# A hybrid convolution, attention and routed feed-forward block: the early plan over two slots, gelu's splits ahead of the weight splits, four batches of picks

## The reference

```python
x = x + _L0_conv_ref(_gn(x), t, weights1, ke_weights, ke_bias)   # group norm, 16 Fourier modes of the channels mixed
t = _to_tokens(x)                                                # 16 sequences of 256 tokens
t = t + _L1_attn_ref(_ln_t(t), W_q, W_k, W_v, W_o)               # causal attention, one head of 256
t = t + _L1_ffn_ref(_ln_t(t), router_w, w_fc, w_proj)

def _L1_ffn_ref(x, router_w, w_fc, w_proj):
    router_probs = jax.nn.softmax(flat_x @ router_w, axis=-1)    # 8 experts
    topk_w, topk_idx = jax.lax.top_k(router_probs, 2)
    topk_w = topk_w / jnp.sum(topk_w, axis=-1, keepdims=True)
    ...
    for e in range(E):
        h = jax.nn.gelu(flat_x @ w_fc[e], approximate=False)     # 256 -> 1024
        out = out + combine[:, e:e + 1] * (h @ w_proj[e])        # 1024 -> 256
```

## Time and profile before

| What | us or share |
|---|---|
| median of three runs | 695.71 |
| profiled execution, its own time | 695.76 |
| its span | 693.9 |
| TensorE (PE) busy | 618.7 (89%) |
| VectorE (DVE) busy | 491.0 (71%) |
| ScalarE (ACT) busy | 412.4 (59%) |
| GpSimd (POOL) busy | 399.6 (58%) |

### The profile page before, as it was taken

The page is one execution under the profiler, slowest core; times in us unless marked ns, Lnnn a source line. Parts: engine busy times, 40 slices in busy tenths (PEclk is TensorE's granted clock), DMA queues, the critical chain, the costliest instruction groups (busy, mean ns, idle before and its releaser), DMA issues. The chain is left out here.

```text
span 693.9 us, 15259 instructions
## 1 busy us (share of the span) xinstructions
PE 618.7 (89%) x4666; PEld 589.3 (85%) x4666; DVE 491.0 (71%) x1190; ACT 412.4 (59%) x720; POOL 399.6 (58%) x292
## 2 busy tenths in 40 slices
PE   1795999999656897779999999999999999999993
PEld 1684888888546897779999999999999999999983
DVE  7663568788756568848778787878787878766661
ACT  2703667775248665567575656666666656656661
POOL 5101121667645577646767667766767676777773
PEclk9997999999898899999999999999999999999998
DMA  8900011224968233676222223231313131312111
GB/s 346 295 4 0 17 35 42 87 102 139 313 226 300 44 87 79 174 264 179 54 38 50 42 42 51 33 59 31 62 31 62 31 62 31 54 26 39 32 25 16
DMA packets 37595, 62.44 MB, mean 90 GB/s; under 512 B 3696, under 2 KB 32944, under 8 KB 36400
## 3 DMA queue, kind: packets, MB, share of 16 engines
q0 software_dynamic: 13296, 18.00, 14.4%
q1 hardware_dynamic: 14816, 34.56, 14.2%
q10 hardware_dynamic: 9440, 9.36, 5.3%
HBM read 37.02 MB, written 24.89 MB: 89 GB/s over the span
## 5 line engine op out<-in xcount | busy, mean ns | idle before, releaser
L679 POOL TENSOR_TENSOR pj_lo<-w_ffn,pj_hi 128x1024 fp32r<-128x1024 f32 x72 | 174.7, 2430 | 96.8 <-ACT pj_hi L746 96.3
L1573 DVE TENSOR_TENSOR fc_lo<-w_ffn,fc_hi 128x1024 fp32r<-128x1024 f32 x78 | 112.8, 1471 | 67.3 <-ACT fc_hi L746 67.3
L746 ACT ACTIVATE pj_hi<-w_ffn 128x1024 fp32r x78 | 82.4, 1060 | 97.7 <-PE psO L1964 76.0
L668 POOL DMA_INDIRECT out<-y,add_id x71 | 114.7, 1616 | 44.6 <-issue 40.6
L1964 PE MATMUL psP<-pj_hi,h_hi 128*128 128x256 f32 x312 | 93.8, 301 | 21.5 <-DVE h_lo L1573 21.5
L746 ACT ACTIVATE fc_hi<-w_ffn 128x1024 fp32r x78 | 79.8, 1055 | 36.3 <-issue 35.6
L1964 PE MATMUL psP<-pj_lo,h_hi 128*128 128x256 f32 x312 | 89.6, 287 | 0.0
L1964 PE MATMUL psP<-pj_hi,h_lo 128*128 128x256 f32 x312 | 89.4, 287 | 0.0
L620 POOL TENSOR_TENSOR roots<-ve,power 128x6 f32<-128x6 f32 (+2 forms) x20 | 23.4, 1172 | 104.3 <-DVE ve L1135 88.3
L630 POOL DMA_INDIRECT slots<-rows,slot x64 | 70.5, 1101 | 18.6 <-issue 17.4
L1964 PEld LDWEIGHTS psP<-pj_hi,h_hi 128*128 128x128 f32 x312 | 60.6, 194 | 24.0 <-issue 22.9
(11 more groups left out here) (365 smaller groups left out, 1608.4 us busy)
## 6 DMA issues: line engine op xcount, KB each, us to landing
w_ffn<-in_w_ffn SPq DMA_DIRECT2D x8, 2048.0 KB, 9.0
xg<-slots ACTq DMA_DIRECT2D x31, 265.0 KB, 3.0
xc<-in_x_ch SPq DMA_DIRECT2D x4, 1024.0 KB, 8.6
out<-x SPq DMA_DIRECT2D x16, 256.0 KB, 2.2
x<-in_x_tok SPq DMA_DIRECT2D x1, 3072.0 KB, 25.0
slots<-fill SPq DMA_DIRECT2D x9, 265.0 KB, 3.0
out<-y,add_id POOLq DMA_INDIRECT x71, 3.9
w_in<-in_w_in SPq DMA_DIRECT2D x1, 1024.0 KB, 13.4
```

Source lines behind the costliest of these rows:

```text
L668: nc.gpsimd.indirect_dma_start(out_d, bass.IndirectOffsetOnAxis(ap=add_id[:, s:s + 1], axis=0), y[:, s, :], None, compute_op=ALU.add).then ...
L679: nc.gpsimd.tensor_tensor(pj_lo[:, 4 * a:4 * a + 4, :], w_ffn[:, bass.ds(e, 1), (2 + a) * DFF:(3 + a) * DFF].rearrange("p a (c d) -> p (a ...
L746: nc.scalar.activation(out, src, ACT.Copy, **kw).then_inc(done, 1)
L1573: v.tensor_tensor(out, whole, upper.bitcast(F32), ALU.subtract).then_inc(done, 1)
```

## The change

- **Four batches of four.** The last batch has eight tiles and all its picking is in the groups; batch 2 ends with sequence 11, so its steps come a slot later. Nothing is picked, counted or weighed in slot 16 any more.
- **Plan.** `order_experts` moves to the middle of slot 12 and loses its last five steps: `order` and `region_at` are now written by ACT, the counts by `order_counts` in slot 13. `first_counts` stands ahead of `conv_out`, `first_rows` (rewritten, seven steps) behind `attn_out`; the four table rows are written by ACT (`first_table`); two constants are set in slot 10.
- **Group 0.** ACT issues its load within slot 14, ahead of `values`. Its transposes stand at the start of TensorE's slot 16, not in slot 15; ACT and VectorE take up their parts accordingly; its first projection split and first gelu run within slot 16.
- **Groups 0 to 5.** ACT does all gelus and casts first and `fc_upper` of the next group behind them, in one piece; VectorE likewise. Group 6's load stands behind chunk 1 of group 5, not at the end of group 4. POOL has five scatters in each group.
- **Tail.** One tail at the end of each group; `plan_rows` is in group 3, `plan_weights` and `half_counts` in group 4, `half_groups` in group 5.

```diff
-BATCHES = (0, 4), (4, 4), (8, 3), (11, 2), (13, 3)
+BATCHES = (0, 4), (4, 4), (8, 4), (12, 4)
...
-            pool.wait_ge(first_ready, 1)
+            pool.wait_ge(first_ready, 4)
...
-                scatter_some(4)
+                scatter_some(5)
...
+            def first_table():
+
+                act.wait_ge(located, 1)
+                copy(table[:, 0, 0:AHEAD], first_at[:, :], first_ready, bias=float(LATE))
+                copy(table[:, 2, 0:AHEAD], first_at[:, :], first_ready, scale=16.0, bias=16.0)
+                act.wait_ge(row_ready, 1)
+                act.wait_ge(order_ready, 2)
+                nc.scalar.activation(table[:, 1, 0:AHEAD], first_plan[:, 0, :], ACT.Identity,
+                                     bias=region_at[:, 0:1]).then_inc(first_ready, 1)
+                nc.scalar.activation(table[:, 3, 0:AHEAD], first_plan[:, 1, :], ACT.Identity,
+                                     bias=expert_at[:, 0:1]).then_inc(first_ready, 1)
+
             def act_slot(k):
+                if k == B:
+                    x_upper(0)
                 if on(k - 1):
                     softmax(k - 1)
...
                     probs_out(k - 1)
+                if k == B:
+                    act.wait_ge(stored_first, 16 * (STORED_FIRST + 1))
+                    proj_upper(0, 0)
+                    for j in batch_at(k - 4):
+                        pick_ratio(j)
+                    gelu(0, 0)
+                    act.wait_ge(stored_next, 16 * (B - 1 - STORED_FIRST))
+                    cast(0, 0)
+                if k == B - 2:
+                    act.wait_ge(first_ready, 4)
+                    act.wait_ge(scattered_early, SENT * EARLY)
+                    act.sem_inc(act_passed, 1)
+                    load_group(act, 0)
                 if on(k):
                     values(k)
...
+                if k == EARLY + 4:
+                    act.wait_ge(sorted_ready, 1)
+                    copy(order[:, :], expert_at[:, :], order_ready)
+                    copy(region_at[:, :], expert_at[:, :], order_ready, scale=float(REGION))
+                if k == EARLY + 5:
+                    first_table()
                 if k == B - 2:
-                    act.wait_ge(first_ready, 1)
-                    act.wait_ge(scattered_early, SENT * EARLY)
-                    act.sem_inc(act_passed, 1)
-                    load_group(act, 0)
                     act.wait_ge(spec_lower, B // 2)
                     fc_upper(0, 0, range(0, 1))
                 if k == B - 1:
                     fc_upper(0, 0, range(1, DH))
-                    x_upper(0)
...
             def act_group(g, par):
                 if relieved(g):
                     proj_upper(g, 1)
                     if g == 1:
                         pick_ratio(len(BATCHES) - 1)
...
+                    for c in range(FC // 2):
+                        if g > 0 or c > 0:
+                            gelu(g, c)
+                            cast(g, c)
+                        if g == 0 and c == 0:
+                            normalise(B - 2, B + 1, 0, rows[:, 2 * B - 4:2 * B - 2, :], xn2_ready)
+                        if g_on(g - 1) and c == 0:
+                            outputs(g - 1)
+                        if g + 1 == AHEAD and c == 1:
+                            load_planned(g + 1)
+                    x_upper(g + 1)
+                    fc_upper(g + 1, 1 - par)
...
             def order_experts():
...
+                v.tensor_reduce(expert_at[:, :], chosen[:, :, :], AX_X, ALU.add).then_inc(sorted_ready, 1)
+
+            def order_counts():
+
+                dve.wait_ge(sorted_ready, 1)
+                known_then(v.tensor_tensor(chosen[:, :, :], placed[:, :, :], over_experts(known[:, :]), ALU.mult))
+                known_then(v.tensor_reduce(known_key[:, :], chosen[:, :, :], AX_X, ALU.add))
+                known_then(v.tensor_tensor(expert_step[:, 0:E - 1], expert_at[:, 1:E], expert_at[:, 0:E - 1], ALU.subtract))
...
+                if k == EARLY + 4:
+                    order_experts()
+                if k == EARLY + 5:
+                    order_counts()
+                    first_counts()
+                if k == B:
+                    proj_lower(0)
...
                 if on(k - 1):
                     attn_out(k - 1)
+                if k == EARLY + 5:
+                    first_rows()
+                if k == B - 1:
+                    fc_lower(0, 0, expert_of(0), range(1, DH))
+                    slot_meta(0)
                 if on(k):
                     highest(k)
...
-                if k == sum(BATCHES[KNOWN]) + 4:
-                    order_experts()
-                if k == sum(BATCHES[KNOWN]) + 5:
-                    first_counts()
-                    first_rows()
...
+            def tail_of(g):
 
                 if g == 0:
                     pick(last, 0)
                     pick(last, 1)
                     gap_scale(last)
                     count_picks(last)
...
                     where_in(last)
                     find_slots(last)
                     counts_out()
+                    weigh(last)
                 if g == 2:
                     plan_ends()
+                if g == 3:
                     plan_rows()
-                if g == 3:
+                    plan_experts()
+                if g == 4:
                     plan_weights()
                     half_counts()
+                if g == 5:
+                    half_groups()
...
+                    if g > 0:
+                        proj_lower(g)
+                    for c in range(FC // 2):
+                        if g == 0 and c == 2:
+                            alone(stored_next, 16 * (B - 1 - STORED_FIRST))
+                            alone(xn2_ready, 2 * B - 2)
+                        hidden(g, c)
+                        if g == 0 and c == 0:
+                            shifts(B + 1)
+                    planned(dve, g + 1)
                     slot_meta(g + 1)
...
                     x_lower(g + 1)
-                    fc_lower(g + 1, 1 - par, e, range(1, DH))
-                    tail_ending(g)
+                    fc_lower(g + 1, 1 - par, expert_of(g + 1))
+                    tail_of(g)
...
                 if k == B:
+                    x_transposes(0)
                     up(0, 0, range(0, 1))
...
-                if k == B - 1:
-                    x_transposes(0)
```

More of the change, by code:

```diff
@@ L888, in cast, with load_planned @@
                 copy(h_hi[:, 2 * c:2 * c + 2, :], hidden_in(g, c), h_hi_ready)
+            def load_planned(g):
+                planned(act, g)
+                if isinstance(g, int) and g == AHEAD:
+                    slots_there(act)
+                    act.wait_ge(idle_stored, 16)
+                act.wait_ge(meta_read, g * 2)
+                act.sem_inc(act_passed, 1)
+                load_group(act, g)
             def act_group(g, par):
@@ L932, in act_group @@
                     gelu(g, 3)
-                if g_on(g + 1):
+                if g_on(g + 1) and not relieved(g):
                     x_upper(g + 1)
[L935 to L943, removed]
+                if g_on(g + 2) and not (isinstance(g, int) and g + 2 == AHEAD):
+                    load_planned(g + 2)
                 if g_on(g + 1):
@@ L1296, in over_experts, with known_then @@
                 return a.unsqueeze(1).broadcast_to([P, E, E])
-            def order_experts():
[L1300 to L1304, removed]
-                    dve.wait_ge(known_step, count[0])
+            count = [0]
+            def known_then(ins):
+                count[0] += 1
+                ins.then_inc(known_step, 1)
+                dve.wait_ge(known_step, count[0])
+            def order_experts():
@@ L1314, in order_experts @@
-                then(v.tensor_tensor(chosen[:, :, :], placed[:, :, :], over_experts(numbers_e), ALU.mult))
-                then(v.tensor_reduce(expert_at[:, :], chosen[:, :, :], AX_X, ALU.add))
-                v.tensor_copy(order[:, :], expert_at[:, :]).then_inc(order_ready, 1)
-                then(v.tensor_scalar(region_at[:, :], expert_at[:, :], float(REGION), None, ALU.mult))
-                then(v.tensor_tensor(expert_step[:, 0:E - 1], expert_at[:, 1:E], expert_at[:, 0:E - 1], ALU.subtract))
@@ L1371, in first_rows @@
-                first_then(v.tensor_reduce(first_expert, first_sum[:, :, some], AX_X, ALU.add))
-                first_then(v.tensor_scalar(first_expert, first_expert, expert_at[:, 0:1], None, ALU.add))
-                v.tensor_copy(table[:, 3, 0:AHEAD], first_expert).then_inc(first_ready, 1)
+                jump = steps_at[:, 0, some]
+                first_then(v.tensor_copy(done[:, 0:1], first_ends[:, 0:1]))
+                first_then(v.tensor_tensor(done[:, 1:n], first_ends[:, 1:n], first_ends[:, 0:n - 1], ALU.subtract))
@@ new lines, in first_rows @@
+                first_then(v.tensor_scalar(jump, expert_step[:, some], float(REGION), None, ALU.mult))
```

(7 more changed lines are left out.)

109 lines of the change are left out of this document (27 added, 82 removed).

## The result

The changed kernel took 701.53 us (median of 6 runs, 700.28 to 707.12), the kernel before 696.49 us in the same session (6 runs, 694.13 to 698.18): a ratio of 1.008, 95% interval 1.0052 to 1.0108. A second session gave 700.21 against 696.94, ratio 1.0068 (1.0034 to 1.0101). The change makes the kernel slower, by 5.0 us in the one session and 3.3 in the other; 688.9 was forecast, 6.9 us faster, with a range up to 699. The profiled execution took 703.84 us, its span is 702.1.

The account below looks back on a forecast made before the run. TensorE alone was taken to set the pace behind group 5, carrying shifts to the end. Group 6's load comes 7.0 us sooner (4.8 from U, 2.2 from the groups), less 0.1: 695.8 - 6.9 = 688.9 us, range 682 to 699.

Parts of the forecast that it names:

- Part 1: Early plan, slots 12 to 14: VectorE's plan steps moved, TensorE's two stalls shrink; alone worth 5 to 6 us.
- Part 2: Group 0's load moved ahead of slot 15: issued at 187.35, U becomes 200.6, 4.8 us sooner.
- the early load takes the stall's place: Rival before slot 15: scatter lands at 190.6 as before, U 204.2, time 692.5; chance 0.20.
- Part 3: Group 0: reordered splits on ACT start group 1 at U + 16.6 and group 2 at U + 32.4.
- Part 4: POOL, groups 0 to 4: 24 scatters at 1.6 us each; last ends at U + 84.4, lands at U + 87.
- The slower rival: POOL, groups 0 to 4: scatters at 1.9 us or more become the bound, 702 us; chance 0.16.
- Part 5: Plan's tail a group later: last write at U + 75, fills landed at U + 89, after the scatters.
- the rule on collisions: VectorE with two SBUF inputs and GpSimd reading SBUF exclude each other for a whole instruction; 2.4 us on the plan's tail.

Follow-up runs that it names:

- plan_at_end: Changed kernel with plan_weights in group 3's tail, half_groups in the wait for group 6's rows, VectorE's early plan steps at ends of slots 12 and 13: 690.86 us.
- before_plan_late: Kernel before the change, with plan_weights, half_counts and half_groups each one group later in the old order: 708.83 us, ratio 1.0153 to the kernel before.
- halves_in_wait: Changed kernel with half_groups moved from group 5's tail into VectorE's wait for group 6's rows: 695.39 us, ratio 0.9985 to the kernel before.
- weights_back: Changed kernel with plan_weights back in the tail of group 3 instead of group 4: 693.88 us, ratio 0.9962 to the kernel before.

## Why the prediction was wrong

U is again the start of group 0's first product, and U + 16.2 a moment 16.2 us behind it.

**Part 1 was right in its mechanism.** The 3.61 us for `where` are gone; 1.24 us for `p_b` are left in that place (0.4 forecast), and `xn`'s stall is 0.92 us (1.2 forecast). Undoing it costs about 3 us of time (plan_at_end), where 5 to 6 at the end of slot 14 were forecast.

**Part 2 was right in one trace only, by luck.** 187.0 was the forecast end of the wait, and ACT's load went out at 187.67 in the first profile:

```profile
182.70 1.03 POOL L633 DMA_INDIRECT slots<-rows,slot  x1 [0.20 <-issue]
...
187.67 0.44 ACTq L444 DMA_DIRECT2D xg<-slots  x1
```

But in the eight further profiles with the same code up to there it went out between 189.14 and 191.17 (mean 190.0), and group 0 started at 204.0 on average, not 200.6. That is the rival "the early load takes the stall's place", with its load at 190.6 and U of 204.2. The term that was wrong is not the way from issue to load: that took 5.0 us in the first profile and 5.9 on average in the eight, with 5.85 forecast and 7.8 before. It is the issue of the last early scatter: forecast at 181.5, it came at 182.70 in the first profile and at 184.1 on average in the eight (183.15 before). The root of slot 13 did not move to 172.8 but stood at 174.06 in the first profile and at 175.1 to 176.0 in the eight. The gain at group 0 was put too high by some 3 us. How much of it is left is uncertain too, as the mark it is counted from is one trace: the kernel before started group 0 at 205.43, and before_plan_late, with the same code up to there, at 208.32.

**Part 3**: group 1 at U + 16.2 (forecast 16.6), group 2 at U + 35.0 (32.4), with 31.9 to 35.1 in the eight other profiles.

**Part 4 was put too dear.** From 211 to 293 us 25 scatters cost 26.0 us and 7.2 of issue time, 1.33 each, not 1.6. The last one ended at U + 81.8, not U + 84.4. The slower rival built on scatters at 1.9 or more fell. Its threshold was also added up wrongly: 24 scatters at 0.3 us more each move U + 87 to U + 94, which is 294.8 and still ahead of the old 296.8.

**Part 5 had the right mechanism and was 3.3 us short.** The fills do come after the scatters. Load of group 6: forecast 289.8, measured 293.13. Of that 0.8 is U, 1.2 the plan's write (U + 76.2, not U + 75; `fc_lo` in front of its steps took 2.35 us in its two parts, 1.3 were charged), 1.4 the way from the write to the load (15.6 us, not 14.2, with 9.54 for the issue of the fills instead of 8.68). Counted from U the load comes at 91.8 and, in the second profile, 89.7, with 91.3 before: between group 0 and this milestone the change gained next to nothing. The rows then took 8.4 us beside the weight load, as forecast. At this milestone the change still gains 3.6 us. One reading of this part was wrong: the scan of 3.10 us does not bear out the rule on collisions as it was cited, since it began at 261.03, 0.67 us ahead of `pj_lo` (261.70). The subtractions do: in the changed kernel's first profile 27 of the 28 `fc_lo` of 128x1024 that began while a `pj_lo` ran took 1.6 to 3.3 us and ended 1.1 us behind it, the 47 that met none took 1.2.

**The step that failed** is the sentence that behind group 5 TensorE alone sets the pace and a shift there is carried unchanged to the end, and with it a line of the diff that no part priced: `half_groups` moves from the early tail of group 4 to the tail of group 5. There it ran from 288.15 to 291.87, and TensorE stood 1.57 us behind it (292.62, for `h_lo`); that was under cover, since TensorE then waited another 3.83 us for group 6's rows, whose time the last scatter set. Here it stands behind the arrival of group 6's rows, between two `fc_lo` on which TensorE waits. The forecast never asked what covers these steps and what they cost without that cover. Fifteen steps of 0.2 us look like 3 us, and with one of them caught by `pj_lo` they made 5.2 (halves_in_wait takes 4.8 off the time). So -3.6 at the load became -3.2 at group 6 and +2.1 at group 7.

The sum over the first profile: the end was forecast 6.9 us sooner and came 8.2 later, 15.1 apart. 3.3 are the load of group 6, 0.5 the way from it to group 6's first product, 5.2 the fifteen steps, 0.5 the groups up to 38 and 5.6 the race at the end. The last is luck, bad this time: without it this execution would have taken about 698, inside the range, though slower than the kernel before and not faster. The medians of 701.5 and 700.2 lie 2 to 3 us above that; in how many runs the race was lost, no trace tells.

**And a term that was priced was not judged.** Part 5 has the plan's tail a group later. Against the old milestone of 296.76 that looked like part of a gain; but the scatters alone would have allowed the load at about 286. weights_back gives 6.3 us for it, before_plan_late 11.2 in the old order. The sum was made for the whole change and never with that one part left out, and so the forecast saw a gain of 7 that the change's other parts had made and this one had already cut.

With both put right the kernel takes 687.8, near the forecast, but for other reasons than its own: group 0 gains less (203.27 against 205.43) and the groups more (the load at U + 83.3, against U + 91.3 before).

## What to carry to other kernels

Where a buffer load waits for several chains, list all of them with their slack, before and after: bringing one forward by 10 us gives only what the next one leaves, and delaying the next one by a step of the pipeline can take it all. Small steps are free only where they stand ahead of a wait; the same fifteen steps just behind it cost 5 us, so such bookkeeping is best put where its engine waits anyway. And price every line of a diff that moves, the unremarkable ones first.

## What was not expected of the hardware

- A subtraction of 1.22 us took 3.29 when it began just behind POOL's `pj_lo`. A shift of 0.24 us between two engines (0.07 ahead, 0.17 behind) decided about 5.3 us at the end, the clock's fall to its lower level included.
- The same code takes different times up to group 4: from group 3's start to group 4's it was 13.3 us in both profiles of the changed kernel and 16.1 in that of halves_in_wait, whose code is the same there. Five of the profiles with four batches have 15.9 to 17.1 us, and in each TensorE stood for 2.8 us there, waiting for `pj_lo`. In halves_in_wait this and what followed put the load of group 6 at 298.09. Of a single profile, differences under 4 us in this stretch prove nothing; the medians do.
- Two milestones of one trace may both be on the lucky side, as the first profile's 187.67 and 201.37 were.
